# A mixture-of-experts assignment whose table of token numbers is made of bf16 products, with each token's weights and experts stored behind its row

## The reference, cut to what matters

```python
def _L0_ffn_ref(x, gate_w, gate_b, w1, b1, w2, b2):      # D 256, H 1024, E 64, K 3, C 128
    xf = x.reshape(-1, D)
    logits = xf @ gate_w + gate_b
    top_l, top_i = jax.lax.top_k(logits, K)
    gates = jax.nn.softmax(top_l, axis=-1)
    fe = top_i.reshape(-1)
    fg = gates.reshape(-1)
    tok = jnp.repeat(jnp.arange(T), K)
    oh = jax.nn.one_hot(fe, E, dtype=jnp.int32)
    pos = (jnp.cumsum(oh, axis=0) * oh).sum(-1) - 1
    valid = pos < C
    buf = jnp.zeros((E, C, D), x.dtype).at[fe, pos].set(xf[tok], mode='drop')
    h = jax.nn.gelu(jnp.einsum('ecd,edh->ech', buf, w1) + b1[:, None, :], approximate=False)
    y = jnp.einsum('ech,ehd->ecd', h, w2) + b2[:, None, :]
    rows = y[fe, jnp.minimum(pos, C - 1)] * (fg * valid.astype(x.dtype))[:, None]
    return jnp.zeros_like(xf).at[tok].add(rows).reshape(x.shape)
...
x = x + 0.5 * _L0_ffn_ref(_layernorm(x), ...)
```

## Time and profile before

| | |
|---|---|
| median of 3 runs | 3115.01 us (3107.58 to 3115.89) |
| the profiled execution | 3107.8 us, its span 3106.1 us |
| busy over the span | PE 91%, PEld 65%, DVE 54%, ACT 50%, POOL 42% |
| mean granted clock of TensorE | 0.951 |

### The profile page before, as it was taken

How to read it: one execution, slowest core, us unless ns; L and a number is a source line. 1 busy time by engine, 2 the same in 40 slices (tenths; PEclk the granted TensorE clock), 3 DMA queues, 4 the chain that set the end, 5 groups by cost and what they waited for, 6 DMA issues and landing times. The chain is left out here.

```text
span 3106.1 us, 54232 instructions
## 1 busy us (share of the span) xinstructions
PE 2824.6 (91%) x19419; PEld 2032.8 (65%) x19419; DVE 1674.6 (54%) x4656; ACT 1556.4 (50%) x2621; POOL 1317.7 (42%) x1315
## 2 busy tenths in 40 slices
PE   6899999877898988588999998999879999998999
PEld 5799999732444443368999996666546566655676
DVE  5411111288888888363111112677776666666666
ACT  1133333369899898311333332333257777783333
POOL 5444444379888888163444442000043443320000
PEclk9899999889999999768999998999989999999999
DMA  8299999705566555862999997000052333301000
GB/s 288 73 327 328 325 329 325 224 16 37 59 60 65 56 62 62 97 201 86 326 325 328 328 326 228 5 1 1 25 133 72 78 98 94 91 1 39 14 14 20
DMA packets 360543, 432.23 MB, mean 139 GB/s; under 512 B 86721, under 2 KB 315238, under 8 KB 357222
## 3 DMA queue, kind: packets, MB, share of 16 engines
q1 hardware_dynamic: 334902, 394.66, 48.0%
q0 software_dynamic: 24576, 33.57, 5.1%
q10 hardware_dynamic: 816, 0.79, 0.1%
HBM read 356.08 MB, written 72.88 MB: 138 GB/s over the span
## 5 line engine op out<-in xcount | busy, mean ns | idle before, releaser
L1806 ACT ACTIVATE f_h_t<-f_h_ps,f_b_t 128x128 f32<-128x128 f32 x1024 | 319.6, 363 | 596.3 <-PE f_h_ps L1764 596.0
L2186 POOL TENSOR_TENSOR a_dmg_buf<-a_c 128x2048 f32<-128x2048 f32 x128 | 519.9, 4096 | 77.8 <-PE a_dmg_ps L2250 48.4
L1764 PEld LDWEIGHTS f_h_ps<-f_rows_t,f_w 128*128 128x128 f32 x4096 | 482.8, 194 | 9.9 <-issue 3.5
L1764 PE MATMUL f_h_ps<-f_rows_t,f_w 128*128 128x128 f32 x4096 | 483.9, 277 | 2.3 <-DVE f_rows_t L1820 1.2
L1778 PE MATMUL f_y_ps<-f_w,f_h_t 128*128 128x256 f32 x2048 | 483.4, 379 | 0.0
L1724 POOL DMA_INDIRECT acc_rows<-f_y,f_give x128 | 205.0, 1602 | 487.6 <-DMA acc_rows<-f_y,f_give 441.1
L1778 PEld LDWEIGHTS f_y_ps<-f_w,f_h_t 128*128 128x128 f32 x2048 | 369.8, 190 | 39.9
L1820 DVE COPY f_rows_t<-f_t_ps 128x256 f32<-128x256 f32 x128 | 54.3, 424 | 597.9 <-PE f_t_ps L1752 597.9
L2562 DVE SCALAR_TENSOR_TENSOR a_bond_buf<-a_a,a_small_rep,a_q_ps 128x512 f32<-128x512 f32 x512 | 346.6, 739 | 8.0 <-PE a_q_ps L2380 4.2
L999 ACT ACTIVATE a_prob<-a_prob,a_neg_top 128x384 f32<-128x384 f32 (+3 forms) x512 | 276.5, 570 | 46.7 <-POOL a_neg_top L816 46.5
L536 DVE SCALAR_TENSOR_TENSOR x_resid<-f_y_ps,f_gate,x_resid 128x256 f32 x512 | 216.7, 478 | 122.5 <-PE f_y_ps L384 111.9
(11 more groups left out here) (358 smaller groups left out, 4135.4 us busy)
## 6 DMA issues: line engine op xcount, KB each, us to landing
f_w<-in_L_ffn_w_dram SPq DMA_DIRECT2D x256, 1024.0 KB
a_skewed<-skew SPq DMA_DIRECT2D x32, 512.0 KB, 6.8
a_k_s<-parts SPq DMA_DIRECT2D x16, 768.0 KB, 7.8
acc_rows<-x_resid SPq DMA_DIRECT2D x17, 512.0 KB, 7.8
xn_rows<-f_xn SPq DMA_DIRECT2D x16, 512.0 KB, 3.6
a_vals<-val_rows SPq DMA_DIRECT2D x64, 128.0 KB, 3.9
skew<-a_bond SPq DMA_DIRECT2D x128, 64.0 KB
x_resid<-acc_rows SPq DMA_DIRECT2D x30, 256.0 KB, 7.0
```

The source lines that it names most:

```text
L1764: last = nc.tensor.matmul(h_ps[n // HB][:, (n % HB) * P:(n % HB + 1) * P], w1_sb[s][:, c, n * P:(n + 1) * P], rows_t[e % 2][:, c, :], star ...
L1806: nc.scalar.activation(h_t[k][:, n, :], h_ps[n // HB][:, (n % HB) * P:(n % HB + 1) * P], ACT.Gelu, bias=b1_t[:, n, e:e + 1]).then_inc(gelu ...
L2186: nc.gpsimd.tensor_tensor(dmg_buf[n % RING][:, :, :], places(c_sb[h], first_place(dg)), c_sb[h][:, PAD:].unsqueeze(1).broadcast_to([P, DG, ...
```

## The change

The table is made of bf16 numbers, which are exact up to 256: a token's number is split into its tile (0 to 31, `tile_number`) and its number within the tile (1 to 128). `place` and `entry` become bf16. POOL writes only the tile numbers into `entry`; ACT writes the numbers within the tile by a copy of `pick` with a scale (`number_tokens`). The weights no longer go through the table. Instead the row of a token in `xn_rows` gets 6 more floats: its three weights and its three experts (`chosen`), stored by SP with a transfer of its own for each batch (`store_chosen`), behind the row store of the batch two later. PE waits for ACT's part as well before a table product. DVE waits, ahead of writing `chosen`, for the store two batches earlier. `read_table` puts the two numbers together. In `experts` the gathered row brings weights and experts along, and DVE picks the one of this expert with a comparison and a sum (`weigh`), two experts ahead.

```diff
-        self.xn = nc.dram_tensor("xn_rows", (B * S, D), FP32, kind="Internal").ap()
+        self.xn = nc.dram_tensor("xn_rows", (B * S, D + 2 * TOP), FP32, kind="Internal").ap()
...
-        expert = sb("expert", [P, TOP, TPB])
+
+        chosen = [sb(f"chosen{k}", [P, TPB, 2, TOP]) for k in range(2)]
...
-        place = [sb(f"place{k}", [P, NK, CAP]) for k in range(2)]
-        entry = [sb(f"entry{k}", [P, NK, 2, E]) for k in range(2)]
+        place = [sb(f"place{k}", [P, NK, CAP], BF16) for k in range(2)]
+        entry = [sb(f"entry{k}", [P, NK, 2, E], BF16) for k in range(2)]
...
+            def store_chosen(i):
+                sp.wait_ge(weight_ready, i + 1)
+                sp.dma_start(sparse.batch(sparse.xn, i)[:, :, D:], chosen[i % 2][:, :, :, :].rearrange("p j w r -> p j (w r)")
+                             ).then_inc(chosen_stored[i % 2], 16)
...
-                sp.dma_start(sparse.batch(sparse.xn, i), xn[i % 2][:, :, :]).then_inc(xn_stored[i % 2], 16)
+                sp.dma_start(sparse.batch(sparse.xn, i)[:, :, 0:D], xn[i % 2][:, :, :]).then_inc(xn_stored[i % 2], 16)
+                if i >= 2:
+                    store_chosen(i - 2)
...
                 nc.gpsimd.tensor_tensor(of[:, :, :, 0, :], pick[k][:, :, :, :],
-                                        number[:, i * TPB:(i + 1) * TPB].unsqueeze(1).unsqueeze(3).broadcast_to([P, TOP, TPB, E]),
-                                        ALU.mult)
-                pool.wait_ge(weight_ready, i + 1)
-                nc.gpsimd.tensor_tensor(of[:, :, :, 1, :], pick[k][:, :, :, :],
-                                        weight[k][:, :, :].unsqueeze(3).broadcast_to([P, TOP, TPB, E]),
+                                        tile_number[:, i * TPB:(i + 1) * TPB].unsqueeze(1).unsqueeze(3).broadcast_to([P, TOP, TPB, E]),
                                         ALU.mult).then_inc(entry_ready, 1)
...
                 pe.wait_ge(entry_ready, i + 1)
+                pe.wait_ge(token_ready, i + 1)
...
+            def number_tokens(i):
+                k = i % 2
+                act.wait_ge(pick_ready, i + 1)
+                if i >= 2:
+                    act.wait_ge(table_done, i - 1)
+                nc.scalar.activation(entry[k][:, :, 1, :], pick[k][:, :, :, :].rearrange("p r j e -> p (r j) e"), ACT.Copy,
+                                     scale=number[:, 0:1]).then_inc(token_ready, 1)
...
-                nc.vector.tensor_copy(expert[:, :, :], top_i[:, :, 0:TOP].rearrange("p j r -> p r j"))
+                if i >= 2:
+                    dve.wait_ge(chosen_stored[i % 2], 16 * (i // 2))
+                nc.vector.tensor_copy(chosen[i % 2][:, :, 1, :], top_i[:, :, 0:TOP])
...
-                nc.vector.tensor_scalar(found[:, :], table_ps[:, 0:E], WHOLE, -WHOLE, ALU.add, ALU.add)
-                nc.vector.tensor_copy(gate[:, :], table_ps[:, E:2 * E])
-                nc.vector.drain()
-                nc.vector.tensor_scalar(empty[:, :], found[:, :], 0.0, number[:, B * TPB:], ALU.is_equal, ALU.mult)
+                nc.vector.tensor_copy(first_number[:, :], table_ps[:, E:2 * E])
+                nc.vector.drain()
+                nc.vector.scalar_tensor_tensor(out=found[:, :], in0=table_ps[:, 0:E], scalar=float(P), in1=first_number[:, :],
+                                               op0=ALU.mult, op1=ALU.add)
+                nc.vector.tensor_scalar(empty[:, :], first_number[:, :], 0.0, number[:, B * TPB:], ALU.is_equal, ALU.mult)
+                nc.vector.drain()
...
-        rows = [sb(f"rows{s}", [P, D]) for s in range(R)]
+        rows = [sb(f"rows{s}", [P, D + 2 * TOP]) for s in range(R)]
...
                     pool.wait_ge(x_turned, e - R + 1)
+                    pool.wait_ge(gate_made, e - R + 1)
...
+            def weigh(e):
+
+                nc.vector.scalar_tensor_tensor(out=share[:, e % 3, :], in0=rows[e % R][:, D + TOP:], scalar=float(e),
+                                               in1=rows[e % R][:, D:D + TOP], op0=ALU.is_equal,
+                                               op1=ALU.mult).then_inc(gate_made, 1)
+                nc.vector.drain()
+                nc.vector.tensor_reduce(gate[:, e % 3:e % 3 + 1], share[:, e % 3, :], AX.X, ALU.add)
...
             for e in range(E):
                 if e + 2 < E:
                     copy_rows(e + 2)
+                    weigh(e + 2)
                 finish(e)
```

More of the change, by code:

```diff
@@ L1298, in route @@
         total = sb("total", [P, 1, TPB])
-        weight = [sb(f"weight{k}", [P, TOP, TPB]) for k in range(2)]
-        place = [sb(f"place{k}", [P, NK, CAP]) for k in range(2)]
-        entry = [sb(f"entry{k}", [P, NK, 2, E]) for k in range(2)]
+        place = [sb(f"place{k}", [P, NK, CAP], BF16) for k in range(2)]
+        entry = [sb(f"entry{k}", [P, NK, 2, E], BF16) for k in range(2)]
+        tile_number = sb("tile_number", [P, B * TPB])
+        first_number = sb("first_number", [P, E])
         empty = sb("empty", [P, E])
@@ L1333, in route @@
         entry_ready = sem("r_entry")
+        token_ready = sem("r_token")
         table_done = sem("r_table")
         block = ctx.enter_context(nc.Block())
+        chosen_stored = [sem(f"r_chosen_stored{k}") for k in range(2)]
         ROOTS = ((0, 1), (1, 2), (2, 4), (4, B))
@@ L1361, in _ @@
                     core.clear(sp, to_clear[i - R])
+            for i in range(B - 2, B):
+                store_chosen(i)
             for k in range(2):
                 sp.wait_ge(xn_stored[k], 16 * (B // 2))
+                sp.wait_ge(chosen_stored[k], 16 * (B // 2))
         @block.gpsimd
@@ L1532, in _ @@
                     copy_turned(i + 2)
+                number_tokens(i)
         @block.vector
@@ L1602, in weigh @@
                 nc.vector.drain()
-                nc.vector.scalar_tensor_tensor(out=weight[k][:, :, :], in0=shifted[:, :, :], scalar=0.5,
+                nc.vector.scalar_tensor_tensor(out=chosen[k][:, :, 0, :].rearrange("p j r -> p r j"), in0=shifted[:, :, :], scalar=0.5,
                                                in1=total[:, :, :].broadcast_to([P, TOP, TPB]), op0=ALU.mult,
@@ L1661, in _, with experts @@
             read_table()
-def experts(core, sparse, name, E, H, R, b1_rows, b1_loaded, w1_sb, w2_sb, b2_row, take, give, gate, acc_stored,
+def experts(core, sparse, name, E, H, R, b1_rows, b1_loaded, w1_sb, w2_sb, b2_row, take, give, acc_stored,
             w_loaded, load_weights):
@@ L1675, in experts @@
         b1_t = sb("b1_t", [P, HC, E])
-        rows = [sb(f"rows{s}", [P, D]) for s in range(R)]
+        rows = [sb(f"rows{s}", [P, D + 2 * TOP]) for s in range(R)]
+        share = sb("share", [P, 3, TOP])
+        gate = sb("gate", [P, 3])
         rows_t = [sb(f"rows_t{k}", [P, DC, P]) for k in range(2)]
@@ L1690, in experts @@
         x_copied = sem("x_copied")
+        gate_made = sem("gate_made")
         h_ready = sem("h_ready")
@@ L1830, in finish @@
                 nc.vector.drain()
-                nc.vector.tensor_scalar(y_sb[k][:, :], y_biased[k][:, :], gate[:, e:e + 1], None,
+                nc.vector.tensor_scalar(y_sb[k][:, :], y_biased[k][:, :], gate[:, e % 3:e % 3 + 1], None,
                                         ALU.mult).then_inc(y_copied, 1)
-            copy_rows(0)
-            copy_rows(1)
+            def weigh(e):
[4 more added lines that the diff above has]
+                nc.vector.tensor_reduce(gate[:, e % 3:e % 3 + 1], share[:, e % 3, :], AX.X, ALU.add)
+            for e in range(2):
+                copy_rows(e)
+                weigh(e)
             for e in range(E):
```

13 lines of the change are left out of this document (7 added, 6 removed).

## The result

Six runs of each kernel, side by side: before 3105.01 us (3098.54 to 3115.89), after 3080.42 us (3075.51 to 3093.05). The ratio is 0.9922 with an interval of 0.9897 to 0.9948: the change made the kernel faster by 0.8%, where the prediction had 0.2% and its range ended at 3085. The prediction took its 6 us off 3115.01 us, the median of the first three of these six runs of before. So of the 28.6 us between its 3109 and the measured 3080.42, 10.0 are its starting point and 18.6 the size of the change: 24.6 us instead of 6. The profiled execution of after took 3093.05 us, the slowest of its six; that will matter.

A forecast was written before the change was run, and what follows sets the result against it. PE was taken to bound routing (at half clock) and experts. Without spells +6 us, four clock spells -12, other terms nothing: net -6 us, so 3115 - 6 = 3109 us, range 3085 to 3124.

The forecast's parts named there:

- the term for the clock spells: Routing loops on PE: two upper-clock spells a stage, 3 us each; four spells -12, with the +6 a net of -6 us.
- a few microseconds: Whole kernel: scatter allowed in the forecast because where a clock spell falls can differ between executions.
- The rival with the clock high once it is up: Routing: clock stays high after rising, -25 to -40 us, kernel 3075 to 3090 us; chance 0.17.
- The price of the product: Routing, PE: twelve bf16 table products take 1.47 us at the lower clock and 0.79 at the upper, priced from L1451.
- the lower bound: Routing, table product: a record halves and each product has one, so 5.23/4 = 1.31 us.
- the terms at nothing: Side effects on POOL, ACT, DVE, SP and gathers: covered by waits or idle time, nothing added to the forecast.
- POOL's lost product: Routing: POOL loses L1404, 1.47 us, as cover since POOL waits for PE; were it the bound, 24 us.
- the small stores: Routing: DVE's new wait for the store two batches earlier is covered by 1 us or more in the slow loop.
- SP's waits for the weights: Routing: weight load and next acc store move behind xn of batch i, both needed tens of microseconds later.
- ACT's copy: Routing: one more copy of 768 elements a batch, 0.59 to 0.88 us, cost 0; all on the path, 14 us.
- DVE's is_equal: Routing: writes bf16 but reads float32; no change taken, at most half of 1.76 us less.
- +36 us for the transfers: Experts: rival that transfers become the bound through wider gathers, +36 us, 3151 us; chance 0.08.

The follow-up runs named there:

- table-four-times run: Changed kernel with 36 more bf16 products of the same shape behind each batch's 12 table products, into unused columns; 3102.18 us, ratio 1.0004 to the kernel before.
- both experiments: Changed kernel with place and entry in float32: 3107.39 us, 0.9991; kernel before with rows of 1048 bytes and small stores of zeros: 3107.48 us, 0.9989.
- second profile: Both kernels profiled again without edit; before 3112.33 us in one run, after 3084.27 us, ratio 0.9911; profiled spans 3110.6 and 3082.6 us.
- wide rows alone: Kernel before with rows of 262 floats gathered whole and six zeros stored behind each row, weights still through the table; 3107.48 us, 0.9989.
- float32 table in the gap: Kernel before with only the order changed: a batch's table products moved ahead of the next logits; 3086.23 us, 0.9918.
- burst and gap: Changed kernel with table products ahead of the next logits, plus 48 constant products before the first prefix counts and 8 in the first turn's gap; 3062.41 us, 0.9879.

## Why the prediction was wrong

**The step that failed is the term for the clock spells**, "I take two spells in a stage", 3 us each, -6 a stage: a spell is a stretch at the upper level. The four loops from the prefix counts of batch 2 to those of batch 6 were forecast at 51.3 us without a spell. Measured: 44.45 and 44.44 us in the first profile (61.86 to 106.31, 1361.37 to 1405.81), 41.80 and 35.48 in the second:

```profile
106.31 0.85 PE L1459 MATMUL f_pos_ps<-f_pick,f_before 128*128 128x256 bf16 x3
...
1405.81 0.85 PE L1459 MATMUL f_pos_ps<-f_pick,f_before 128*128 128x256 bf16 x3
```
```profile
61.39 0.85 PE L1459 MATMUL f_pos_ps<-f_pick,f_before 128*128 128x256 bf16 x3
...
103.19 0.85 PE L1459 MATMUL f_pos_ps<-f_pick,f_before 128*128 128x256 bf16 x3
...
1366.75 0.85 PE L1459 MATMUL f_pos_ps<-f_pick,f_before 128*128 128x256 bf16 x3
...
1402.23 0.49 PE L1459 MATMUL f_pos_ps<-f_pick,f_before 128*128 128x256 bf16 x3
```

A loop that is all at the lower level took 12.64 us for 12.83. Against four of these the first profile gained 6.1 us by spells in each stage, as forecast, and did so in two short ones (10 us of upper level). The second gained 8.8 us in one spell of 13.7 us, and 15.1 us in three, with 24 us of upper level within the loops. So two spells of 3 us were right for the slowest of six executions; in the one at the median the spells were worth 23.9 us in both stages instead of 12. Of the 22.4 us that its routing is shorter than before, 6 are the forecast, 11.9 the spells beyond it, and the other 4.5 the cheaper table and the stages' ends.

**The change of clock was given no spread of its own.** The text says that where a spell falls can differ "a few microseconds". In the kernel before it hardly does (107.4 to 108.3 us in four stages); in the changed kernel it does, by 12.4 us between two executions. The table-four-times run points at the reason: what was removed is the 5 us of dense work behind which the level came back whenever it had fallen. The rival with the clock high once it is up gave 3075 to 3090 and a chance of 0.17. Its number is the one that came, by a mechanism between it and the forecast: the level still falls two or three times in a stage of the better profile. The range took in only part of it and ended 5 us short. That much hangs on the starting point, too: 24.6 us off the 3115 that the forecast started from is 3090, inside the range, so it is the three runs of before, the slower half of the six, together with the spells that put the result outside.

**The price of the product** was right in kind and high by a sixth: 1.25 us for 1.47 at the lower level, 0.68 for 0.79 at the upper. L1451 was too dear a row, for a reason that no run shows; the lower bound, a fourth of 5.23, was nearer. It is 0.057 us a product at the upper level. For the upper level 2.94 us was read as the float32 table's time; that is the record's length, and from start to start it is 2.78. The Trainium skill (TensorE: Matmul & The Clock Gate, LDWEIGHTS) has 0.107 us for the load of each, and the trace stays against it; the same page (Wait — 56ns, not 53.3ns?) has 55.6 ns for products back to back, and with that the trace agrees.

**The wait that the prediction read past** is the 0.78 us between transposes and logits. It says that the clock "fell again in the logits" each time (it did six times of eight; the last spell of each stage outlasted the stage), and doesn't ask what stands ahead of them. Moving the table into it gained alone what the change gained alone. The Trainium skill (TensorE: Matmul & The Clock Gate, A second HAM failure mode: psum-queue depth-cycling) tells of a kernel in which frequent short idle times between groups of products let the clock swing between its levels; here the level went behind such a wait at 1366 us (the first timeline above), and held for 33 us with it nearly filled, but the fall at 1349 us came with 0.11 us of waits in the 10 us ahead of it, which that section doesn't explain.

**Right were** the terms at nothing. POOL's lost product and the small stores: both experiments within 0.3% of before. DVE never waited for a store in routing, and SP's waits for the weights (up to 12.3 us) had nobody behind them. ACT's copy took 0.94 us against at most 0.88, in its idle time; POOL's product took 1.61 us in the first stage and 1.47, as before, in the second and in both of the second profile. DVE's is_equal kept its 1.76 us (1.76 to 1.81). In the experts DVE's wait ahead of `finish` went from 1.31 to 0.99 us and the loop stayed at 7.25 us, so +36 us for the transfers is refuted: with wide rows alone 0.9989. PE waited 5.3 us for gathered rows in the second pass of the first profile, but not at all in the second profile; in the kernel before, the first expert of a pass left out, not at all in one profile and 1.0 and 1.8 us in the other. That is part of the scatter between executions.

**Left open**: what makes the level fall where PE is busy throughout, and so how long a spell lasts; and why it rises at 56 us in one execution and at 69 in another behind the same work. With the float32 table in the gap it lasted 61 us in the first stage and 48 in the second, with the short one 10 to 27 in the same order (37 once, in burst and gap), which points at the work in the loop (the table's share of it, or its type) rather than at waits; that wasn't tried by itself.

## What to carry to other kernels

- Where an engine's clock depends on its own work, price an edit by the level it leaves behind as well as by the time it takes away (here, in the second stage, the table gave 21.6 to 21.9 us and the rest took 12.1 back in one execution, 3.3 in another), and ask of the work that is cut whether it was what lifted the level. Give the level's spread its own term in the range.
- Read the small waits of the bounding engine in each loop and put independent work into them before shortening anything: here moving a product into a wait of 0.78 us gave 0.8% alone, and 1.2% with the change (3064 us against 3099). It is the version to keep; neither filler at the start nor at the end added to it measurably. How much of the 1.2% is the wait itself and how much the level isn't settled by the medians.
- One profile of such a kernel isn't enough, nor are three runs: the first profile of the changed kernel was its slowest of six, and read alone it would have confirmed the forecast's spells; the three runs that the forecast started from lay 10 us above the median of six.

## What the hardware showed unexpectedly

- 36 products into unused columns, three quarters of a table's work, put the clock's pattern in the first stage back to that of the float32 table to 0.3 us (prefix counts at the upper rate from 65.24 against 65.01 us).
- With a float32 table in the gap, the second stage's level rose at 1366.5 and stayed up until 1414.3 us; with the bf16 table there (the same loop, shorter) it fell at 1349.2 and again at 1376.5 us.
- 48 products on constants lifted the level at 42 us, some 27 us early; PE had been at work for 16 us before them without a rise. The same in the other three stages that had them, 24 to 25 us into the stage instead of 39 to 51.
